# The end of a graph attention kernel: one order of the last elementwise steps against another, with the x - 1 made beforehand on GpSimd

## What is computed

```
h  = max(layernorm(x), 0)
h  = h @ W1 + b1
e  = leaky_relu((h @ a1)[:, None] + (h @ a2)[None, :] + b2, 0.2)
A  = softmax(where(adj > 0, e, -1e12), axis=1)
out = x + elu(A @ h)
```

## Time and profile before

| | us |
|---|---|
| median of 3 runs | 435.43 (435.4 to 436.04) |
| the profiled execution, its own time | 435.46 |
| its span in the trace | 433.6 |
| TensorE busy | 411.1 (95%) |
| VectorE busy | 384.1 (89%) |
| ScalarE busy | 316.8 (73%) |
| GpSimd busy | 35.7 (8%) |
| mean granted TensorE clock | 0.995 of full speed |

### The profile page before, as it was taken

One profiled execution on the slowest core, in us unless ns is written; L12 is line 12 of the kernel. 1 busy time (PEld: TensorE's weight loads), 2 busy tenths in 40 slices (PEclk: granted clock), 3 DMA queues, 4 the chain that ended last, 5 costly groups with the idle time before them and its releaser, 6 DMA issues.

```text
span 433.6 us, 8603 instructions
## 1 busy us (share of the span) xinstructions
PE 411.1 (95%) x3375; PEld 408.0 (94%) x3375; DVE 384.1 (89%) x405; ACT 316.8 (73%) x312; POOL 35.7 (8%) x97
## 2 busy tenths in 40 slices
PE   0789989999999999999999999999999999999995
PEld 0688979999999999999999999999999999999995
DVE  3999889999999579999999299999994799999944
ACT  2678899999997388958765788967664879586522
POOL 2334200000000030000000300000000300000003
PEclk9999989999999999999999999999999999999999
DMA  8940015466555706655557436548388066566302
GB/s 271 385 182 1 0 38 203 168 214 210 213 210 205 289 5 232 251 195 193 243 184 266 182 112 254 215 132 303 110 317 295 14 241 236 195 212 243 126 5 93
DMA packets 22360, 80.68 MB, mean 186 GB/s; under 512 B 1472, under 2 KB 14016, under 8 KB 14144
## 3 DMA queue, kind: packets, MB, share of 16 engines
q1 hardware_dynamic: 21920, 79.70, 52.1%
q10 hardware_dynamic: 416, 0.66, 0.5%
HBM read 76.15 MB, written 4.19 MB: 185 GB/s over the span
## 4 chain that ended last, share of the span: by engine, by line
PE 88%; DVE 7%; ACT 2%; DMA 2%; issue 0%; POOL 0%; SPq 0%; ACTq 0%; DVEq 0%
PE ps L615 51%; PE ps L617 26%; PE ps L637 2%; PE ps L638 2%; PE ps L639 2%; DVE stats L677 2%; DMA x_s<-x 2%; DVE hnT_lo L704 1%; PE ps L543 1%; DVE h_raw L713 1%; PE ps L545 1%; PE ps L544 1%; DVE xn L694 1%; PE ps L531 1%; ACT h_raw L451 1%; DVE adj_s L751 1%
## 5 line engine op out<-in xcount | busy, mean ns | idle before, releaser
L615 PE MATMUL ps<-hp_hi,w_hi 128*128 (+1 forms) x944 | 230.1, 283 | 1.6 <-DVE hp_lo L881 1.0
L617 PE MATMUL ps<-hp_lo,w_hi 128*128 (+1 forms) x944 | 229.8, 283 | 0.0
L751 DVE SCALAR_TENSOR_TENSOR adj_s<-R,p,adj_s 128x1024 f32<-128x1024 f32 x128 | 165.0, 1329 | 24.5 <-ACT adj_s L395 24.4
L615 PEld LDWEIGHTS ps<-hp_hi,w_hi 128*128 128x128 f32 x944 | 179.3, 190 | 2.0 <-issue 1.2
L617 PEld LDWEIGHTS ps<-hp_lo,w_hi 128*128 128x128 f32 x944 | 179.2, 190 | 0.0
L403 ACT ACTIVATE w_hi<-adj_s 128x2048 fp32r<-128x2048 f32 x64 | 122.4, 1913 | 39.4 <-DVE adj_s L751 39.2
L761 DVE SCALAR_TENSOR_TENSOR w_lo<-adj_s,w_hi 128x2048 fp32r<-128x2048 f32 x64 | 145.9, 2280 | 0.1
L395 ACT ACTIVATE adj_s<-adj_s 128x2048 f32<-128x2048 int32 x64 | 122.3, 1911 | 20.3 <-DMA adj_s<-adj_t 20.0
L615 PE MATMUL ps<-hp_hi,w_lo 128*128 (+1 forms) x944 | 123.0, 283 | 0.0
L615 PEld LDWEIGHTS ps<-hp_hi,w_lo 128*128 128x128 f32 x944 | 117.3, 189 | 0.0
L331 POOL TENSOR_TENSOR y<-y,h_sum 128x2064 f32<-128x2064 f32 x3 | 12.8, 4256 | 273.0 <-ACT y L467 273.0
(11 more groups left out here) (92 smaller groups left out, 265.6 us busy)
## 6 DMA issues: line engine op xcount, KB each, us to landing
adj_s<-adj_t SPq DMA_DIRECT2D x64, 1024.0 KB, 4.8
x_s<-x SPq DMA_DIRECT2D x8, 512.0 KB, 10.5
o_s<-x SPq DMA_DIRECT2D x3, 1024.0 KB, 7.6
out<-o_s SPq DMA_DIRECT2D x6, 512.0 KB, 6.9
adj_s<-x SPq DMA_DIRECT2D x1, 1024.0 KB, 5.5
out<-adj_s SPq DMA_DIRECT2D x8, 128.0 KB, 1.7
vec<-vectors ACTq DMA_DIRECT2D x1, 384.5 KB, 6.4
W1x<-W ACTq DMA_DIRECT2D x1, 256.0 KB, 4.3
```

Of the source, the lines that this page charges most:

```text
L615: last = pe.matmul(acc, block_w, hh, start=fresh, stop=False)
L617: pe.matmul(acc, block_w, hl, start=False, stop=False)
L751: last = dve.scalar_tensor_tensor(sgn, R[:, ds(ic * CW, CW)], p[:, ds(source(r, c) + s, 1)], sgn, ALU.max, ALU.mult)
```

## The change

Three things are different in the end of the last chunk.

- GpSimd takes 1 off x_end in place, bank by bank in 8 instructions (128x256), as soon as x_end has been loaded. It does nothing per bank any more. VectorE waits for all 8 before its first bank.
- For each bank VectorE does, in this order and each behind a wait for the one before: reciprocal; z = rden * ps (PSUM to SBUF, into the buffer o_s, which the earlier chunks' outputs used); o = max(z, 0) + o, with o = x - 1 in x_end; o = min(e, 1) + o. No step of a bank is issued ahead of the bank in front.
- ScalarE makes e = exp(z) from z in SBUF, with no scale, once z is there.

All 8 stores wait for the last VectorE operation of their bank (o_end). max(z, 0) + (x - 1) + min(exp(z), 1) equals x + elu(z).

```
+        z_end_s = o_s
...
             for ib in range(BANKS):
-                if ib < BANKS - 1:
-                    sp.wait_ge(o_end, ib + 1)
-                else:
-                    sp.wait_ge(o_last, 1)
+                sp.wait_ge(o_end, ib + 1)
                 sp.dma_start(out_v[:, (CHUNKS - 1) * BANKS + ib, :], x_end[:, ib, :]).then_inc(stored_end, 16)
...
             pool.wait_ge(x_end_in, 16)
-            for ib in range(BANKS - 1):
-                o = x_end[:, ib, :]
-                pool.wait_ge(elu_end, ib + 1)
-                pool.tensor_tensor(o, e_end[:, ib, 0:F], o, ALU.add).then_inc(o_end, 1)
+            for ib in range(BANKS):
+                pool.tensor_scalar(x_end[:, ib, :], x_end[:, ib, :], -1.0, None, ALU.add).then_inc(x_less, 1)
...
             for ib in range(BANKS):
-                act.wait_ge(rd_end, ib + 1)
-                act.activation(e_end[:, ib, 0:F], ps[:, ib, 0:F], ACT.Exp, scale=rden[:, ib:ib + 1]).then_inc(e_end_ready, 1)
+                act.wait_ge(z_end, ib + 1)
+                act.activation(e_end[:, ib, 0:F], z_end_s[:, ib, :], ACT.Exp).then_inc(e_end_ready, 1)
...
-            def begin_end(ib):
+            def bank_end(ib):
+
                 if ib < BANKS - 1:
                     dve.wait_ge(bank_done, (CHUNKS - 1) * (BANKS - 1) + ib + 1)
                 else:
                     dve.wait_ge(pe_done, CHUNKS * PAIRS)
                 dve.reciprocal(rden[:, ib:ib + 1], ps[:, ib, F:F + 1]).then_inc(rd_end, 1)
+                z, o, e = z_end_s[:, ib, :], x_end[:, ib, :], e_end[:, ib, 0:F]
+                dve.wait_ge(rd_end, ib + 1)
+                dve.tensor_scalar(z, ps[:, ib, 0:F], rden[:, ib:ib + 1], None, ALU.mult).then_inc(z_end, 1)
+                dve.wait_ge(z_end, ib + 1)
+                dve.scalar_tensor_tensor(o, z, 0.0, o, ALU.max, ALU.add).then_inc(xo_end, 1)
+                dve.wait_ge(e_end_ready, ib + 1)
+                dve.wait_ge(xo_end, ib + 1)
+                dve.scalar_tensor_tensor(o, e, 1.0, o, ALU.min, ALU.add).then_inc(o_end, 1)
 
             dve.wait_ge(summed, 2 * CHUNKS - 1)
-            dve.wait_ge(x_end_in, 16)
-            begin_end(0)
+            dve.wait_ge(x_less, BANKS)
+            dve.wait_ge(stored, (CHUNKS - 1) * 32)
             for ib in range(BANKS):
-                if ib + 1 < BANKS:
-                    begin_end(ib + 1)
-                e = e_end[:, ib, 0:F]
-                dve.wait_ge(e_end_ready, ib + 1)
-                dve.tensor_scalar(e, e, 1.0, -1.0, ALU.min, ALU.add).then_inc(em_end, 1)
-                dve.wait_ge(em_end, ib + 1)
-                dve.scalar_tensor_tensor(e, ps[:, ib, 0:F], rden[:, ib:ib + 1], e, ALU.mult, ALU.max).then_inc(elu_end, 1)
-                if ib == BANKS - 1:
-                    o = x_end[:, ib, :]
-                    dve.wait_ge(elu_end, BANKS)
-                    dve.tensor_tensor(o, e, o, ALU.add).then_inc(o_last, 1)
+                bank_end(ib)
```

More of the change, by code:

```diff
@@ L220, in build @@
         e_end_ready = sem("e_end_ready")
-        em_end = sem("em_end")
-        elu_end = sem("elu_end")
+        x_less = sem("x_less")
+        z_end = sem("z_end")
+        xo_end = sem("xo_end")
         o_end = sem("o_end")
-        o_last = sem("o_last")
         stored = sem("stored")
```

## The result

The changed kernel takes 436.91 us (median of 7), the kernel before 435.40 in the same runs: a ratio of 1.0031, interval 1.0019 to 1.0042. It is **slower by 1.5 us**, 0.35% by the medians. I had forecast 435.0, in a range of 434.7 to 436.4. In what follows, single executions of 1416 us (experiment 5), 2268 us (experiment 7) and 581 us (the kernel before, beside experiment 11) were disturbed and are left out of the ratios.

A forecast was written before the change was run, and what follows sets the result against it. TensorE was busy 411.1 of 433.6 us, so the change could act behind the last matmul or by delaying TensorE's inputs. 0.45 (chain) + 0.05 (store) less 0.07 (rhythm, exponential) is 0.43 earlier: 435.0, range 434.7 to 436.4.

The forecast's parts named there:

- Part 1, the chain of one bank: VectorE's serial steps from reciprocal to last operation take 1.61 us; at bank 7 the last operation ends 0.45 earlier.
- Part 2, the rhythm: VectorE's period per bank is 1.53 us against TensorE's 1.54: it just fits, and lateness at bank 0 is not made up.
- the sum: Whole kernel: 0.45 + 0.05 = 0.50 us earlier, less 0.07 for the rhythm and the exponential: 0.43, giving 435.0.
- the exponential decides: Rival in the bank chain: a slow exponential makes the period 1.58, adding 0.3 us at bank 7: 435.2 to 435.4; chance 0.25.
- Part 3, the stores: At the end, the last store may land in 1.7 us instead of 1.8; taken as 0.05, ends 0 and 0.1.
- Part 4, the x - 1 on GpSimd: Before bank 0, GpSimd's eight instructions take turns with VectorE and finish at 418.28, 0.2 us before the first reciprocal.
- Back to back I take 0.42 apart: Before bank 0, the assumed pace of GpSimd's instructions: one every 0.42 us, so the five running alone take 5 x 0.42.
- L342's 0.72: Upper end for one GpSimd instruction of x - 1: the 0.72 us of its existing two-input addition; 0.47 was taken.
- the 0.29 for 128 columns in the earlier trace: GpSimd single-input instructions: 0.23 us for 4 columns, 0.29 for 128, carried on to 0.36 for 256.
- GpSimd comes late: Rival at VectorE's wait for all 8 before bank 0: 0.67 us apart, 1.3 slower, 436.7; chance 0.17.

The follow-up runs named there:

- experiment 5: Changed kernel with x - 1 made on ScalarE in one instruction behind its last weights, instead of GpSimd's eight: 435.35 us, ratio 0.9998 to the kernel before.
- experiment 7: Changed kernel with VectorE waiting bank by bank for GpSimd's x - 1 and only once before each last operation: 435.39 us, ratio 0.9996 to the kernel before.
- experiment 11: Changed kernel with GpSimd's x - 1 in four instructions of 128x512 and one wait before each last operation: median 435.36 us, ratio 1.0018 to the kernel before.
- experiment 4: Changed kernel with one semaphore, so one wait instead of two, before each bank's last operation: 436.37 us, ratio 1.0041 to the kernel before.
- Experiment 9: Changed kernel with GpSimd's eight instructions subtracting a tile of ones (two inputs) instead of adding a constant: 437.47 us, ratio 1.0047 to the kernel before.
- experiment 8: Changed kernel with GpSimd's x - 1 as one instruction of 128x2048 instead of eight: 439.05 us, ratio 1.0070 to the kernel before.

## Why the prediction was wrong

**Part 1, the chain of one bank: right.** z took 0.48, the followers 0.42 and 0.42 and the exponential 0.42, against 0.48, 0.42, 0.42 and 0.40 to 0.47. The chain was 1.66, not 1.61, and the 0.05 is the second wait in front of the last operation, for which I had taken the 0.04 of a single one. It gives back 0.40, where I had 0.45.

**Part 2, the rhythm: right in kind, its size off by that same wait.** I worked out 1.53 against TensorE's 1.54 and found that lateness is not made up. It was 1.59, so 0.40 were added over 7 banks, where the sum has 0.07 for it. The rival for this, "the exponential decides", had the size (0.3) and the wrong cause: experiment 4 took the wait away and left the exponential, and the rhythm fell to 1.52.

**Part 3, the stores: right**: the last lands in 1.7 instead of 1.8, the upper end of my 0 to 0.1.

**Part 4, the x - 1 on GpSimd: the step that failed.** Its picture held in every point but one. The engines took turns, three before w_lo was done, the hold was 0.15 to 0.20 (I took 0.25), and w_lo ended at 416.06 (I took 416.18) with TensorE unharmed. The failed term is "Back to back I take 0.42 apart": it was 0.84. From 416.06 the five remaining instructions took 3.97, not 2.10, and the eighth was done at 420.03, not 418.28: bank 0 began 1.6 late instead of not at all. With the second wait (0.40, of which the sum had 0.07) that makes the miss of 1.9. I had got the 0.42 by giving a one-input instruction half of what L342 needs above the fixed part. Experiment 9 shows that this is false in sign: alone, its two-input form is the faster of the two. My upper end, L342's 0.72, wasn't an upper end either, because L342 is another form; nor was the 0.29 for 128 columns in the earlier trace rows, a third form, a guide to the slope. The rival "GpSimd comes late" was what happened, in place and mechanism. That its 436.7 lies so near 436.91 is partly luck: its hold (0.5, measured 0.2) and TensorE's stall (0.3, measured none) were too large, its pace (0.67) too small, and it had no loss in the rhythm. Its chance of 0.17 was too little, and the range ended at 436.4, inside that rival, instead of beyond it.

The Trainium skill's "GPSIMD Engine Reference", section 3.1, gives 1.03 cycles per element for a light body; by it, with the 0.23 of the earlier trace rows as the fixed part, one instruction would take an estimated 0.45. The measurement, 0.84, decides. The rule of "SBUF — State Buffer", section "Who interferes with whom", that the two engines exclude each other, agrees with the masks and w_lo, stretched by 0.15 to 0.20 a turn. That the other engine is shut out for the whole instruction agrees less, as far as records show it: a one-input instruction whose record is 0.84 held VectorE for 0.2, and the one pass with a record of 5.50 held it for 3.4.

## What to carry to other kernels

Work that is moved to an idle engine "beforehand" has a deadline, and the deadline is the consumer's first wait: price its pace by a row of the same form and size, count the turns it has to wait for, and let the consumer wait piece by piece, not for the whole. Where the consumer's period is as long as its producer's, any lateness at its start arrives at the end in full, and one more wait per step (0.06 here) can decide whether it catches up. Look for an engine whose idle stretch lies before the deadline and whose work the others don't feel: here ScalarE took the same work in 1.90, with w_lo at 4.48 as without it, and the time of the kernel without the - 1 (435.35 against 435.37).

## What the runs showed that I had not expected

- GpSimd's addition of a constant to 256 columns takes 0.84 alone, its subtraction of two tensors 0.74. One pass of 2048 took 5.50. Some 0.24 of it was waiting for the first mask, which took 1.27 and ended at 409.88; 5.26 less 0.84 for 1792 columns more is 2.5 ns a column.
- How long a GpSimd instruction holds a VectorE instruction with two SBUF inputs: one input 0.15 to 0.20 for 256 columns, 0.36 to 0.42 for 512, 3.4 for 2048; two inputs 0.50 to 0.55 for 256.
- A second wait in front of a VectorE instruction, met at about the same time as the first, costs 0.06 to 0.07.
- In experiment 8 TensorE stood idle for 2.11, and its granted clock fell to 0.50 a microsecond after it had taken up work again, for some 3.4 us. It cost 1.5 us.
